# Masked attention in a four-part Trainium2 kernel: the weighing of the values moves in front of the next tile's scores, and the first half's turned probabilities move behind them

## The reference, cut to what matters

```python
# per batch b: 2048 queries, 128 keys, 16 heads of 32
x = x + _L1_xattn_ref(_layernorm(x), ctx, ctx, mask, ...)

Q = split_heads(q @ Wq.T + bq); K = split_heads(k @ Wk.T + bk); V = split_heads(v @ Wv.T + bv)
scores = einsum('bhqd,bhkd->bhqk', Q, K) / sqrt(32)
scores = where(mask, 1e-09, scores)
attn = softmax(scores)
ctx = einsum('bhqk,bhkd->bhqd', attn, V)
return ctx @ Wo.T + bo
```

## Time and profile before

| | us |
|---|---|
| median of 3 runs (lowest, highest) | 1520.21 (1519.3, 1521.04) |
| the profiled execution | 1522.23 |
| its span, first to last instruction | 1520.4 |
| PE busy in the span | 1453.4 (96%) |
| DVE busy | 1204.9 (79%) |
| ACT busy | 880.0 (58%) |
| POOL busy | 505.1 (33%) |

### The profile page before, as it was taken

The page is one execution under the profiler, slowest core; times in us unless marked ns, Lnnn a source line. Parts: engine busy times, 40 slices in busy tenths (PEclk is TensorE's granted clock), DMA queues, the critical chain, the costliest instruction groups (busy, mean ns, idle before and its releaser), DMA issues. The chain is left out here.

```text
span 1520.4 us, 30089 instructions
## 1 busy us (share of the span) xinstructions
PE 1453.4 (96%) x10634; PEld 1073.8 (71%) x10634; DVE 1204.9 (79%) x2421; ACT 880.0 (58%) x2090; POOL 505.1 (33%) x442
## 2 busy tenths in 40 slices
PE   7899999999999999899998998999999999998996
PEld 5677777777777777644443467888888877776885
DVE  5688888897888765688878977888888896786775
ACT  2444444444444443655567847888888876763442
POOL 0122222222222221200003744455555654664333
PEclk9999999999999999999999999999999999998998
DMA  8411111110111101122305710000000024225641
GB/s 298 177 47 45 45 45 45 45 41 8 38 41 35 45 8 77 46 124 115 143 1 230 289 41 3 3 1 3 3 4 3 3 85 178 114 100 189 190 149 59
DMA packets 47807, 118.34 MB, mean 78 GB/s; under 512 B 9422, under 2 KB 15950, under 8 KB 46032
## 3 DMA queue, kind: packets, MB, share of 16 engines
q1 hardware_dynamic: 42016, 100.03, 18.8%
q0 software_dynamic: 5680, 16.85, 2.8%
HBM read 78.90 MB, written 39.80 MB: 78 GB/s over the span
## 5 line engine op out<-in xcount | busy, mean ns | idle before, releaser
L1840 ACT ACTIVATE c_probs<-c_score,c_minus_top 128x128 f32<-128x128 f32 x512 | 183.8, 421 | 4.7 <-DVE c_minus_top L1976 4.6
L1790 POOL TENSOR_TENSOR c_probs<-c_probs,c_recip 128x1024 f32<-128x1024 f32 x64 | 121.7, 1901 | 163.6 <-DVE c_recip L1982 163.6
L700 POOL TENSOR_TENSOR a_attn_lo_parts<-a_attn,a_attn_hi_parts 128x512 fp32r<-128x512 f32 x64 | 80.6, 1294 | 250.3 <-ACT a_attn_hi_parts L762 250.3
L1840 ACT ACTIVATION_READ_ACCUMULATOR c_probs<-c_score,c_minus_top 128x1 f32 x512 | 133.4, 260 | 0.0
L758 ACT COPY a_attn<-a_pv_ps 128x512 f32<-128x512 f32 x64 | 37.0, 578 | 164.4 <-PE a_pv_ps L1060 164.4
L1467 POOL TENSOR_TENSOR xres<-xres,b_delta 128x512 f32<-128x512 f32 x24 | 48.4, 2029 | 209.4 <-DVE b_delta L1524 209.4
L430 PE MATMUL a_bank<-a_x_hi_parts,a_wq_hi 128*128 128x256 f32 x512 | 106.9, 290 | 0.3 <-PEq L445 0.3
L430 PE MATMUL a_bank<-a_x_lo_parts,a_wq_hi 128*128 128x256 f32 x512 | 103.1, 283 | 0.0
L430 PE MATMUL a_bank<-a_x_hi_parts,a_wq_lo 128*128 128x256 f32 x512 | 102.8, 282 | 0.0
L1028 PE MATMUL a_bank<-a_wo_hi,a_attn_hi_parts 128*128 128x512 f32 x248 | 99.5, 401 | 0.0
L1030 PE MATMUL a_bank<-a_wo_hi,a_attn_lo_parts 128*128 128x512 f32 x248 | 98.1, 395 | 0.0
(11 more groups left out here) (358 smaller groups left out, 4335.1 us busy)
## 6 DMA issues: line engine op xcount, KB each, us to landing
hidden<-b_hidden SPq DMA_DIRECT2D x5, 2816.0 KB, 8.1
b_hidden<-hidden SPq DMA_DIRECT2D x5, 2816.0 KB, 10.6
xres<-in_x SPq DMA_DIRECT2D x8, 1024.0 KB, 14.3
d_we<-in_we SPq DMA_DIRECT2D x8, 1024.0 KB, 6.9
xres<-in_w_gate_up SPq DMA_DIRECT2D x7, 1024.0 KB, 5.4
d_got<-rows SPq DMA_DIRECT2D x20, 258.0 KB, 2.9
xres<-rows SPq DMA_DIRECT2D x19, 258.0 KB, 3.0
a_rot<-in_rot SPq DMA_DIRECT2D x16, 256.0 KB, 3.1
```

Source lines behind the costliest of these rows:

```text
L700: nc.gpsimd.tensor_tensor(of_spread(attn_lo, g), of_spread(attn, g), of_spread(attn_hi, g), ALU.subtract).then_inc(attn_lo_ready, 1)
L1790: nc.gpsimd.tensor_tensor(part, part, recip[:, t % 2, heads].unsqueeze(2).to_broadcast([P, HALF, KEYS]), ALU.mult).then_inc(scaled, 1)
L1840: last = nc.scalar.activation(probs[:, t, at, :], score_ps[:, h, g, :], ACT.Exp, bias=minus_top[:, h, g:g + 1], accum_out=total[:, t, at:a ...
```

## The change

On PE, W (with its tile's number as before) now stands directly in front of the scores S of the next tile, behind Qb, L and T; PT0 and PT1 of the current tile stand behind these scores instead of in front of them. `plan` puts W behind T. On ACT, the 16 exponentials of a tile are no longer parted by `attn_high`; that follows behind Qb, T and L. On DVE, `attn_low` goes from behind the statistics to behind `x_low`, the last place of a step. In the last chunk `gate_exponentials` on ACT moves in front of `attn_high`, and `gate_top` on DVE in front of `x_low`. The very first step (tile 0) stays as it was, and no instruction is added, dropped or resized.

```diff
@@ plan
-                for what in (...) if g == 0 else ("Qa", "PT2", "PT3", "O", "W", "Qb", "L", "T", "PT0", "PT1"):
+                for what in (...) if g == 0 else ("Qa", "PT2", "PT3", "O", "Qb", "L", "T", "W", "PT0", "PT1"):
@@ scalar
-                            for h in range(2 if isinstance(n, int) and tile == 1 else 0, 3):
+                            for h in range(2 if isinstance(n, int) and tile == 1 else 0, 4):
                                 exponentials(tile, t, h)
-                        if "W" in s:
-                            attn_high(here("W"))
-                        if t < NT:
-                            exponentials(tile, t, 3)
                         if "Qb" in s:
                             queries(1 - j, 2 * t + 1, here("Qb").full, here("Qb").out)
                         if "T" in s:
                             x_high(tile + 2 * NT, j, t, here("T").full, here("T").out)
+                        if "L" in s:
+                            if t == 1:
+                                act.wait_ge(freed["gate"], gate_use[0].emptied[1])
+                            gate_exponentials(t).then_inc(freed["gate"], 1)
+                        if "W" in s:
+                            attn_high(here("W"))
...
-                            if t == 0:
-                                gate_exponentials(0).then_inc(freed["gate"], 1)
                             if t == 1:
-                                act.wait_ge(freed["gate"], gate_use[0].emptied[1])
-                                gate_exponentials(1).then_inc(freed["gate"], 1)
                                 gate_norm(TPC)
@@ vector
-                        if "W" in s:
-                            attn_low(use(n, j, t, "W"), tile - 1)
                         if "O" in s:
                             row_stats(use(n, j, t, "O"), tile - 2)
                         if s["N"]:
                             norm_row(tile + 2 * NT + 1, (t + 1) % 2)
                         if t < NT:
                             invert(tile, t, 1)
+                        if "L" in s:
+                            dve.wait_ge(bank_full, gate_use[t].full)
+                            gate_top(t)
                         if "T" in s:
                             x_low(tile + 2 * NT, j, t, use(n, j, t, "T").out)
+                        if "W" in s:
+                            attn_low(use(n, j, t, "W"), tile - 1)
...
-                        if isinstance(n, int) and n == LAST and t < NT:
-                            dve.wait_ge(bank_full, gate_use[t].full)
-                            gate_top(t)
@@ tensor
                             output(here("O"), use(n, j, t - 1, "W"))
+                        if "Qb" in s:
+                            project(begin(here("Qb")), 1 - j, 2 * t + 1)
+                        if "L" in s:
+                            ...
+                        if "T" in s:
+                            turn_x(tile + 2 * NT, t, begin(here("T")))
                         if "W" in s:
                             ...
-                        if "Qb" in s:
-                            project(begin(here("Qb")), 1 - j, 2 * t + 1)
-                        if "L" in s:
-                            ...
-                        if "T" in s:
-                            turn_x(tile + 2 * NT, t, begin(here("T")))
-                        if "PT0" in s:
-                            pe.wait_ge(scaled, 2 * tile + 1)
-                            for h in (0, 1):
-                                turn_probs(here(f"PT{h}"), t, h)
                         if t < NT - 1:
                             scores(b, tile + 1, j, t + 1)
                         elif t == NT - 1 and left(n):
                             pe.wait_ge(freed["act"], here("Qb").emptied[1])
                             scores(b_next, tile + 1, 1 - j, 0)
+                        if "PT0" in s:
+                            pe.wait_ge(scaled, 2 * tile + 1)
+                            for h in (0, 1):
+                                turn_probs(here(f"PT{h}"), t, h)
```

More of the change, by code:

```diff
@@ L1664, in plan @@
                 at = {}
-                for what in ("PT0", "PT1", "Qa", "Qb", "T") if g == 0 else ("Qa", "PT2", "PT3", "O", "W", "Qb", "L", "T", "PT0", "PT1"):
+                for what in ("PT0", "PT1", "Qa", "Qb", "T") if g == 0 else ("Qa", "PT2", "PT3", "O", "Qb", "L", "T", "W", "PT0", "PT1"):
                     if here[what]:
@@ L2243, in body @@
                             output(here("O"), use(n, j, t - 1, "W"))
+                        if "Qb" in s:
+                            project(begin(here("Qb")), 1 - j, 2 * t + 1)
+                        if "L" in s:
+                            if t == 0:
+                                pe.wait_ge(experts.wg_lo_ready, KB)
+                            gate(t, begin(here("L"))[:]).then_inc(bank_full, 1)
+                        if "T" in s:
+                            turn_x(tile + 2 * NT, t, begin(here("T")))
                         if "W" in s:
@@ L2251, in body @@
                             gate(3, score_bank[1]).then_inc(experts.out_full, 1)
-                        if "Qb" in s:
-                            project(begin(here("Qb")), 1 - j, 2 * t + 1)
-                        if "L" in s:
-                            if t == 0:
-                                pe.wait_ge(experts.wg_lo_ready, KB)
-                            gate(t, begin(here("L"))[:]).then_inc(bank_full, 1)
-                        if "T" in s:
-                            turn_x(tile + 2 * NT, t, begin(here("T")))
-                        if "PT0" in s:
-                            pe.wait_ge(scaled, 2 * tile + 1)
-                            for h in (0, 1):
-                                turn_probs(here(f"PT{h}"), t, h)
                         if t < NT - 1:
```

## The result

| | us |
|---|---|
| before, median of 5 runs (lowest, highest) | 1519.62 (1518.66, 1521.04) |
| after, median of 5 runs (lowest, highest) | 1527.06 (1525.98, 1528.5) |
| ratio, 95% interval | 1.0046 (1.0035 to 1.0057) |
| profiled execution after, and its span | 1528.5, 1526.7 |

The change made the kernel slower by 0.35 to 0.57%. The forecast was 1526.5 us, slower, and the two profiled executions differ by 1528.5 - 1522.23 = 6.3 us, the sum of the prediction. The medians differ by 7.4 us.

The account below looks back on a forecast made before the run. A loop through PE and ACT, not PE's own work, was taken as the bound. Terms 6.2 - 0.9 + 0.1 + 0.4 + 0.5 = +6.3 us on 1522.23 gave 1528.5 profiled, 1526.5 as median; range 1518.5 to 1534.5.

Parts of the forecast that it names:

- PT0 and PT1, +0.79 us a tile: Between scores and Qa on PE: eight transposes moved into the PE-ACT loop add 0.79 us a tile.
- the small wait for `x_low`: Qa of a t = 0 step no longer waits for x_low of the step before: -0.10 us every second tile.
- `attn_high`, -0.47: On ACT, attn_high leaves the loop by moving out of the exponentials: -0.47 us a tile, at most -0.67.
- The 26 periods, +6.2: Scores at 956.03 to 1236.86: 280.83 us become 287.0, at 22.01 us a chunk plus 0.89 for a half-clock score group.
- First tiles, -0.9: Qb and T no longer queue behind W's wait for PT3's copy at 928.48: -0.9 us, between 0 and -1.2.
- The next two periods, +0.1: From 932.43 to 956.03: first period 10.49 to 10.82 us, second still set by router constants; +0.1 us.
- the clock, +0.4: Near 954.30: a longer wait before the scores leaves PT0 and PT1 slow inside the loop; +0.4 us, 0 to +0.8.
- Last chunk, +0.5 out of -2.4 to +2.5: Last chunk: PT2's 2.41 us wait for the gate's exponentials goes, but PT1 waits there; +0.5 us taken.
- PE as the pace-maker: Rival: ACT finishes before PE ends W, so periods become PE's own 10.22 us; -14.2 us, about 1506; chance 0.11.
- The moves do not cancel: Denies the rival that attn_high's full 0.67 offsets the transposes' 0.79 in the loop: about 1521 us, chance 0.14.
- DVE is not the pace-maker: Denies the rival that a later attn_low uses up DVE's 0.44 us cover before masking: 9.4 us lost, 1536, chance 0.12.
- A clock that falls again and again: Rival: longer waits before the scores drop PE's clock, stretching PT0, PT1 and scores 0.7 to 0.9 us each; chance 0.05.

Follow-up runs that it names:

- the kernel with W back: The changed kernel with W put back behind O on PE, attn_high and attn_low in front of x_high and x_low: 1526.34 us, ratio 1.0026.
- the kernel with two passes more: The changed kernel with two unused 128x512 bn_stats passes on DVE behind attn_low, for tiles 2 to 27: 1545.03 us, ratio 1.0161.
- the split: The changed kernel with PT0 in front of the next scores and PT1 behind them: 1517.85 us, ratio 0.9984.
- the last kernel: The changed kernel with W back behind O, and PT0 in front of the scores, PT1 behind: 1522.52 us, ratio 1.0006.

## Why the prediction was right

**What bounds the kernel.** It named a loop over PE and ACT, not PE's own work. Right: PE's waits in front of S grew by 0.7 us in either period, and the kernel slowed while PE's busy time fell; with the transposes back in front the first exponential returned to 4.24 us.

**PT0 and PT1, +0.79 us a tile, and the small wait for `x_low`, -0.10 in every second tile.** Together +0.74 a tile, measured alone 0.78. Both kinds of period start their exponentials at 5.06 us in after, where before it was 4.25 and 4.35, so the wait went, and the transposes by themselves cost about 0.82. **`attn_high`, -0.47.** Measured 0.50. Two errors of 0.03 us thus cancel, and that the sum came out as 22.01 us to the hundredth is luck. **W, 0.** Right in the loop, by the kernel with W back.

**The 26 periods, +6.2.** Measured 286.48 - 280.83 = +5.65. In this the half-clock score group of before is not there any more, which the forecast had left in both (-0.89); without it the forecast would have been 13 x 22.01 = 286.1, and the measured stretch is 0.4 us longer, since the second period was 11.27 instead of 11.19 us in four chunks of the first batch.

**First tiles, -0.9.** From the second to the third scores 932.78 - 919.95 = 12.83 us, 13.77 before: -0.94. **The next two periods, +0.1, and the clock, +0.4.** This step failed in its sign: 956.07 - 932.78 = 23.29 us against 23.60, -0.31. The first period came as told (10.82 us), the second is 12.47 instead of 13.11. The forecast held it fixed by the router constants, but they delay only the first exponential (6.36 us behind S, 6.20 before); from there to the next S it is 6.11 us instead of 6.91, of which 0.50 is `attn_high`'s and the rest that the transposes, slow in before, no longer stand in front of these scores. And no half clock followed: PE waited 2.30 us in front of the scores at 956.07, longer than the 1.82 after which it had fallen before, and the scores took 1.17 us. The term that assumed a fall behind a longer wait was wrong by 0.4 in this kernel, and the 26 periods by the 0.89 left in them. The mechanism itself is real: with PT0 and PT1 moved alone the clock fell in this same place, inside the loop, and cost 1.5 us.

**Last chunk, +0.5 out of -2.4 to +2.5.** Measured up to the last W: 34.53 us against 1269.28 - 1236.86 = 32.42 before, +2.11. The two parts named both came: PT2's waits for the gate's exponentials went, 2.41 us and a second one of 0.37, and PT1's of 1.32 and 2.66 took their place. A half-clock stretch follows the 2.41 us before and the 2.66 us after. S to S is 10.72 us instead of 11.22, a part that the prediction did not name: before, PT2 waited 0.91 us for POOL's scaling there, and in after it does not. The size was missed by 1.6 us, inside the bounds.

**Sum.** 5.65 - 0.94 - 0.31 + 2.11 + 0.08 (between the first two scores) = +6.59 us from the first scores to the last W. The rest is outside the change: the stage began 1.21 us later (906.49 against 905.28), behind the same instructions, and what follows the last W was 1.50 us shorter, together +6.3. Over all kernels here the first scores started between 904.55 and 907.88, so a profiled execution is good for about 1.5 us either way. The forecast's median, 0.6 us off, is nearer than that allows to claim, and it leaned on a before of 1520.21; from median to median the change was forecast as +6.3 us and measured as +7.4.

**The rivals.** PE as the pace-maker (1506) fell: no kernel here had both periods near 10.2 us, and in all with a transpose behind S PE waits for ACT in front of the scores, at least in every second tile. The moves do not cancel, 0.78 against 0.50. DVE is not the pace-maker; with 1.2 us more it becomes one. A clock that falls again and again did not come with waits of 1.0 us in front of every second S, nor with 1.3; with 1.7 to 2.2 us, in the kernel with two passes more, it fell three times in the second half of the stage.

## What to carry to other kernels

What a moved instruction costs is set by the loop it enters, not by its engine's load: eight transposes on an engine that waits 0.35 us in front of every second group of scores cost their whole 0.78 us, because they went between the scores and what ACT waits for. Before filling a wait with moved work, follow from the end of the wait to the next instruction that the other engine needs, and look who had the moved work's buffer last; of eight transposes the four whose bank was free early were free, the four whose bank was not were dear. When a move loses, try half of it.

## What was not expected of the hardware

- The granted clock did not follow the length of a single wait: it fell behind waits of 1.82 us (before) and of 1.72 and 0.28 (the split), and stayed at full behind one of 2.30 us (after) and behind nine of 1.73 to 1.82 us (two passes more). Behind 2.46 and 2.64 us (PT0 and PT1 moved; two passes more) the scores ran at full clock in 1.17 us and the fall came 1.6 us after they started. What tells these cases apart the runs do not show.
- One of 10 runs of the last kernel took 2867.5 us, the other nine 1521.04 to 1526.68. It stays unexplained.
- The second period of after was 11.27 us four times in the first batch and 11.18 to 11.20 later, with the same instructions. Why was not looked into.
